# Second product of the attention terms on GpSimd, and the value matmuls turned around onto two column halves of TensorE

## The reference, cut to what matters

```
scores = q @ k.T / 8                      # 1024 x 1024, for each of 8 x 8 = 64 heads
scores = where(chaos(scores), scores / PHI, scores)
attn   = softmax(scores)
attn   = attn * (sin(C1 * attn) * exp(-attn * attn / PHI) + cos(C2 * attn))
ctx    = attn @ v ;  h = h + ctx @ Wo + bo
```

## Time and profile before

| | us |
|---|---|
| runs: median (lowest to highest) of 3 | 6793.55 (6787.77 to 19916.96) |
| the profiled execution | 6774.6 |
| its span, first to last instruction | 6772.9 |
| busy in the span: PE / VectorE / ScalarE / GpSimd | 5442.1 / 5082.3 / 4262.2 / 2754.5 |

### The profile page before, as it was taken

One profiled execution on the slowest core, in us unless ns is written; L12 is line 12 of the kernel. 1 busy time (PEld: TensorE's weight loads), 2 busy tenths in 40 slices (PEclk: granted clock), 3 DMA queues, 4 the chain that ended last, 5 costly groups with the idle time before them and its releaser, 6 DMA issues. The chain is left out here.

```text
span 6772.9 us, 115321 instructions
## 1 busy us (share of the span) xinstructions
PE 5442.1 (80%) x32426; PEld 3955.2 (58%) x32489; DVE 5082.3 (75%) x10177; ACT 4262.2 (63%) x7370; POOL 2754.5 (41%) x2639
## 2 busy tenths in 40 slices
PE   2788877787777877877888777778787799997999
PEld 1455555555555555555655555555555577775777
DVE  1888888888888888888888888888888555555443
ACT  1677777777777777777777777777777322222222
POOL 4445554444555544444555444445554200100111
PEclk9888898989889888888888889888988799898999
DMA  1000000000000000000000000000000000000000
GB/s 17 12 8 7 7 7 7 7 7 10 7 7 7 7 7 7 7 9 9 7 7 7 7 7 7 9 9 7 7 7 4 8 1 2 1 1 13 4 6 6
DMA packets 34500, 48.46 MB, mean 7 GB/s; under 512 B 24473, under 2 KB 24537, under 8 KB 34010
## 3 DMA queue, kind: packets, MB, share of 16 engines
q1 hardware_dynamic: 31962, 43.49, 2.5%
q0 software_dynamic: 2048, 0.14, 0.1%
HBM read 39.40 MB, written 4.19 MB: 6 GB/s over the span
## 5 line engine op out<-in xcount | busy, mean ns | idle before, releaser
L571 PE MATMUL banks<-ident,att 128*128 128x128 f32 x8192 | 1458.9, 311 | 873.6 <-DVE ag L508 496.8
L571 PEld LDWEIGHTS banks<-ident,att 128*128 128x128 f32 x8192 | 1024.2, 159 | 1568.6 <-DVE ag L508 1044.0
L377 POOL TENSOR_TENSOR sinb<-sinb,work 128x512 f32<-128x512 f32 x1024 | 1289.3, 1272 | 900.3 <-DVE sinb L482 898.3
L599 PE MATMUL banks<-kT,qT 128*128 128x512 f32 x2048 | 1262.5, 702 | 113.9 <-ACT att L423 104.0
L387 POOL TENSOR_SCALAR wgt<-wgt 128x512 f32<-128x512 f32 x1024 | 700.2, 684 | 1586.7 <-DVE wgt L502 1581.4
L635 PEld LDWEIGHTS outp<-vo,sinb 128*128 128x128 f32 x8192 | 1164.7, 216 | 214.9 <-issue 185.3
L635 PE MATMUL outp<-vo,sinb 128*128 128x64 f32 x8192 | 1162.6, 295 | 1.9 <-ACT att L423 1.9
L476 DVE TENSOR_TENSOR work<-banks,work 128x512 f32<-128x512 f32 x1024 | 699.8, 689 | 254.0 <-ACT work L435 183.6
L451 ACT ACTIVATE work<-banks 128x512 f32<-128x512 f32 x1024 | 609.9, 596 | 420.4 <-PE banks L571 411.6
L458 ACT ACTIVATE mag<-banks 128x512 f32<-128x512 f32 x1024 | 606.4, 594 | 356.2 <-PE banks L599 350.0
L435 ACT ACTIVATE work<-banks,halfpi 128x512 f32<-128x512 f32 x1024 | 695.4, 685 | 208.9 <-PE banks L571 139.6
(11 more groups left out here) (194 smaller groups left out, 6740.6 us busy)
## 6 DMA issues: line engine op xcount, KB each, us to landing
xq<-xT_dram SPq DMA_DIRECT2D x64, 256.0 KB
xv<-xT_dram SPq DMA_DIRECT2D x64, 256.0 KB, 3.7
xT_dram<-xT SPq DMA_DIRECT2D x8, 256.0 KB, 2.9
out<-hres SPq DMA_DIRECT2D x8, 256.0 KB, 2.6
base<-in_L_tok_turns,idx POOLq DMA_INDIRECT x64
wqk<-in_L_attn_Wq SPq DMA_DIRECT2D x64, 16.0 KB
wqk<-in_L_attn_Wk SPq DMA_DIRECT2D x64, 16.0 KB
wqk<-in_L_attn_bq SPq DMA_DIRECT2D x64, 0.2 KB
```

The lines of the kernel that those rows point to most:

```text
L377: nc.gpsimd.tensor_tensor(sinb[:, k % RING], sinb[:, k % RING], work[:, k % RING], ALU.add).then_inc(summed, 1)
L571: mm = nc.tensor.matmul(bank[:, i * P:(i + 1) * P], att[:, p, 4 * half + i, kt * P:(kt + 1) * P], ident[:], is_transpose=True, start=(i == ...
L599: nc.tensor.matmul(score_bank(n), qT[:, p, (n // 2) * P:(n // 2 + 1) * P], kT[:, p, (n % 2) * 512:(n % 2 + 1) * 512], start=True, stop=Tru ...
```

## The change

- `sinb` gets ScalarE's sine directly (it was left in the bank), GpSimd multiplies it by `ag` (SBUF times SBUF) in place of its sum, and VectorE's product of sine and `ag` is gone. `fill(k)` of the sine part now waits for ScalarE's sine of tile k-4.
- The sum of the two terms is not formed: `work` (cosine term) and `sinb` (sine term) both go through TensorE as the moving operand, 512 columns each, with `vo` (64 columns) stationary, into partitions 0 to 63 and 64 to 127 of `outp`. The result is transposed and lies in two halves; VectorE moves it into `acc` (a copy for even heads, an addition for odd ones), and after every second head eight matmuls with `pair` (two identities, one above the other) turn it back and add its halves; then VectorE adds it to `hres`.
- The order of the tiles is `kt` first within a query half (it was half first within `kt`), so `outp` holds one half of the queries at a time and is emptied twice a head, at steps 86 and 103. The value matmuls sit at steps 78 to 85 (one a step) and 88 to 102 (one every second step).
- `kT` has one buffer, its rows shared by the two parities; so the projections move from steps 18 and 20 to 24 and 26, the `vo` work from step 25 (of stage 1) to 29.

```
-        kT = sb("kT", [P, 2, S])
+        kT = sb("kT", [P, S])
+        acc = sb("acc", [P, 2, 512])
+        pair = sb("pair", [P, D])
...
-        PROJ, VAL = 18, 25 + STEPS
+        PROJ, VAL = 24, 29 + STEPS
-        AV = [SINE + 6 + 8 * k // 5 for k in range(NTILE)]
-        OUT = AV[-1] + 1
+        AV = [SINE + 6 + k if k < TB else SINE + 16 + 2 * (k - TB) for k in range(NTILE)]
+        OUT = (AV[TB - 1] + 1, AV[-1] + 1)
+        FOLD, ADD = OUT[1] + 1, OUT[1] + 2
...
# GpSimd
-                        k = a - SINE - 5
+                        k = a - SINE - 4
-                            wait(pool, tmul, NTILE * g + k + 1)
-                            nc.gpsimd.tensor_tensor(sinb[:, k % RING], sinb[:, k % RING], work[:, k % RING],
-                                                    ALU.add).then_inc(summed, 1)
+                            wait(pool, sined, NTILE * g + k + 1)
+                            wait(pool, agd, NTILE * (g + 1))
+                            nc.gpsimd.tensor_tensor(sinb[:, k % RING], sinb[:, k % RING], ag[:, k],
+                                                    ALU.mult).then_inc(tmul, 1)
...
# ScalarE, projections
-                    wait(act, qk, NTILE * (g - 1))
+                    wait(act, qk, NTILE * g)
-                nc.scalar.activation(qT[0:D, p, cols], outp[0:D], ACT.Copy, scale=QSCALE).then_inc(qk_sb, 1)
-                nc.scalar.activation(kT[0:D, p, cols], outp[D:P], ACT.Copy).then_inc(qk_sb, 1)
+                rows = slice(p * D, (p + 1) * D)
+                nc.scalar.activation(qT[rows, p, cols], outp[0:D], ACT.Copy, scale=QSCALE).then_inc(qk_sb, 1)
+                nc.scalar.activation(kT[rows, cols], outp[D:P], ACT.Copy).then_inc(qk_sb, 1)
...
# ScalarE, cosine and sine
-                                wait(act, summed, NTILE * g + k - RING + 1)
+                                wait(act, av, NTILE * g + k - RING + 1)
...
-                            nc.scalar.activation(sine_bank(k), sine_bank(k), ACT.Sin,
+                            wait(act, av, NTILE * g + k - RING + 1)
+                            nc.scalar.activation(sinb[:, k % RING], sine_bank(k), ACT.Sin,
...
# VectorE
-                        k = a - SINE - 4
-                            wait(dve, sined, NTILE * g + k + 1)
-                            wait(dve, av, NTILE * g + k - RING + 1)
-                            nc.vector.tensor_tensor(sinb[:, k % RING], sine_bank(k), ag[:, k],
-                                                    ALU.mult).then_inc(tmul, 1)
-                        if a == OUT:
-                            wait(dve, av, NTILE * (g + 1))
+                        if a in OUT:
+                            half = OUT.index(a)
+                            wait(dve, av, NTILE * g + TB * (half + 1))
+                            if p == 0:
+                                nc.vector.tensor_copy(acc[:, half], outp[:]).then_inc(evac, 1)
+                            else:
+                                nc.vector.tensor_tensor(acc[:, half], outp[:], acc[:, half], ALU.add).then_inc(evac, 1)
+                        if a == ADD and p == 1:
+                            wait(dve, folded, folds(g, p) + 1)
...
# TensorE
-                            wait(pe, turned, TB * (g + 1))
-                            kt, half = k // 2, k % 2
+                            wait(pe, turned, TB * g + 4 * (k // TB) + 4)
+                            kt, half = k % TB, k // TB
...
-                            fill(g, p, gauss_bank(d), d // 2, d % 2)
+                            fill(g, p, gauss_bank(d), d % TB, d // TB)
...
-                                wait(pe, tmul, NTILE * g + k - 3)
-                            fill(g, p, sine_bank(k), k // 2, k % 2)
+                                wait(pe, sined, NTILE * g + k - 3)
+                            fill(g, p, sine_bank(k), k % TB, k // TB)
...
-                            for i in range(4):
-                                o = (4 * half + i) * D
-                                mm = nc.tensor.matmul(outp[:, o:o + D], sinb[:, k % RING, i * P:(i + 1) * P],
-                                                      vo[:, kt, :], start=(k == 0 and i == 0),
-                                                      stop=(k >= NTILE - 2), skip_group_check=True)
+                            if k == TB:
+                                wait(pe, evac, 2 * g + 1)
+                            for term, rows in ((work, slice(0, D)), (sinb, slice(D, P))):
+                                mm = nc.tensor.matmul(outp[rows], vo[:, kt, :], term[:, k % RING],
+                                                      start=(kt == 0), stop=(kt == TB - 1), skip_group_check=True)
                             mm.then_inc(av, 1)
+                        if a == FOLD and p == 1:
+                            wait(pe, evac, 2 * g + 2)
+                            for j in range(TB):
+                                mm = nc.tensor.matmul(outp[:, j * D:(j + 1) * D],
+                                                      acc[:, j // 4, j % 4 * P:(j % 4 + 1) * P], pair[:],
+                                                      start=True, stop=True)
+                            mm.then_inc(folded, 1)
```

More of the change, by code:

```diff
@@ L277, in lattice @@
         names = ("consts loadq loadv projd qk_sb vald v_sb qk mags rounded kept factor filtered bias expd "
-                 "recip weights weights2 turned xpose squared gauss agd cosd acd nned sined tmul summed av outd").split()
+                 "recip weights weights2 turned xpose squared gauss agd cosd acd nned sined tmul av evac folded outd").split()
         (consts, loadq, loadv, projd, qk_sb, vald, v_sb, qk, mags, rounded, kept, factor, filtered, bias,
-         expd, recip, weights, weights2, turned, xpose, squared, gauss, agd, cosd, acd, nned, sined, tmul, summed,
-         av, outd) = (sem("l_" + n) for n in names)
+         expd, recip, weights, weights2, turned, xpose, squared, gauss, agd, cosd, acd, nned, sined, tmul,
+         av, evac, folded, outd) = (sem("l_" + n) for n in names)
         NTILE = 2 * TB
@@ L316, in stages, with folds @@
                     yield g, (par - stage) % 2, s + STEPS * stage
+        def folds(g, p):
+            if isinstance(g, int):
+                return g // 2
+            return (g - p) // 2
         def score_bank(n):
@@ L365, in _ @@
             pool.wait_ge(consts, 5)
-            nc.gpsimd.memset(qT[D:P], 0.0).then_inc(consts, 1)
+            nc.gpsimd.tensor_tensor(pair[:], ident[:, 0:D], ident[:, D:P], ALU.add).then_inc(consts, 1)
             pool.wait_ge(consts, 6)
-            nc.gpsimd.memset(kT[D:P], 0.0).then_inc(consts, 1)
+            nc.gpsimd.memset(qT[:], 0.0).then_inc(consts, 1)
+            pool.wait_ge(consts, 7)
+            nc.gpsimd.memset(kT[:], 0.0).then_inc(consts, 1)
             def iteration(t, par):
@@ L393, in _ @@
         def _(act):
[L394 removed]
+            act.wait_ge(consts, 8)
             def projections(g, p, c):
@@ L447, in iteration @@
                             if d < RING:
-                                wait(act, summed, NTILE * g - RING + d + 1)
+                                wait(act, av, NTILE * g - RING + d + 1)
                             else:
@@ L507, in iteration @@
                             wait(dve, gauss, NTILE * g + d + 1)
+                            wait(dve, tmul, NTILE * (g - 1) + d + 1)
                             nc.vector.tensor_tensor(ag[:, d], gauss_bank(d), work[:, d % RING],
@@ L549, in _, with project @@
         def _(pe):
-            pe.wait_ge(consts, 7)
-            def project(g, c):
+            pe.wait_ge(consts, 8)
+            def project(g, p, c):
                 wait(pe, loadq, 80 * (g + 1))
                 if c == 0:
-                    wait(pe, outd, g - 2)
+                    wait(pe, evac, 2 * (g - 2))
+                    wait(pe, outd, folds(g - 2, p))
                 else:
@@ L560, in project @@
                 nc.tensor.matmul(outp[:], wqk[:], xq[:, c * 512:(c + 1) * 512], start=True, stop=True).then_inc(projd, 1)
-            project(0, 0)
-            project(0, 1)
+            project(0, 0, 0)
+            project(0, 0, 1)
             def fill(g, p, bank, kt, half):
@@ L597, in iteration @@
                             if n == 3:
-                                wait(pe, tmul, NTILE * (g - 2) + 13)
+                                wait(pe, sined, NTILE * (g - 2) + 13)
                             nc.tensor.matmul(score_bank(n), qT[:, p, (n // 2) * P:(n // 2 + 1) * P],
-                                             kT[:, p, (n % 2) * 512:(n % 2 + 1) * 512],
+                                             kT[:, (n % 2) * 512:(n % 2 + 1) * 512],
                                              start=True, stop=True).then_inc(qk, 1)
@@ L610, in iteration @@
                             if d < 3:
-                                wait(pe, tmul, NTILE * (g - 1) + 14 + d)
```

(26 more changed lines are left out.)

3 lines of the change are left out of this document (1 added, 2 removed).

## The result

7027.28 us (7018.53 to 7039.49, 4 runs) against 6790.66: a ratio of 1.0353 [1.0331, 1.0375], slower. (One of the four runs of the kernel before took 19916.96 us; it is in the median of 6790.66 and left out of the ratio.) The forecast was 7060 in a range of 6740 to 7350. The total came out; its terms did not, and their errors mostly cancelled.

What follows compares the result with a forecast made beforehand. VectorE was taken to bound the scores and gauss part, a ring of four PSUM banks the sine part. Terms of +3.4, +0.5, +1.0, +0.34 and -0.6 gave +4.6 us a head, +288 over 62 heads: 7060 us, range 6740 to 7350.

Steps and rivals of the forecast that it cites:

- ring and pairs in the sine part: Sine part: eight steps with value matmul pairs at 2.05 us, three without at 1.25, +3.4 us a head; ninth pair +0.5.
- moved work: Projection copies and `vo` matmuls at later steps, around the sine part's start: +1.0 us a head, between 0 and +3.1.
- emptying, fold, GpSimd: Mostly the VectorE-bound stretch: emptying and residual +0.34 us a head, fold 0 (or +0.95), shorter first rounding -0.6.
- The bound by stretch: VectorE full in scores and gauss part, no engine in the sine part; removing VectorE's 702 us pays only there.
- The pairs: TensorE, sine part: two value matmuls into column halves take 1.29 us plus 0.08 for the change of kind, 1.37.
- only the second and the third record can run together: TensorE, a pair's four records of 0.43 us: one overlap only, so 3 x 0.43 = 1.29 us.
- The signs: Head about 84 us; sine fills 2.0 us apart at eight steps, else 1.25; records at 0, 0.43, 0.43, 0.86; TensorE never idle.
- Fully together: Rival, value pairs on TensorE: both halves overlap completely, 0.86 us a pair, +0.9 us a head, 6830 us; chance 0.20.
- In turn: Rival, value pairs on TensorE: halves do not overlap, 1.72 us a pair, +8.6 us a head, 7310 us; chance 0.28.
- The ring set free: Rival, sine part: pairs at most 0.54 us, GpSimd sets 1.25 us a tile, -3.2 us a head, 6575 us; chance 0.12.

Runs made afterwards that it cites:

- the kernel with one half: Changed kernel with both value terms summed into the same column half of `outp` (partitions 0 to 63), same output: 7475.21 us.
- its best form: Changed kernel with the moved work in its old steps, `mag2` of three buffers and seven PSUM banks in the sine part's ring: 6794.88 us, ratio 1.0025.

## Why the prediction was right, and where it was not

The slower kernel was forecast, and the total of 7060 was near; but that is luck in good part. Put by stretches, with the kernel with the moved work put back as the step between, a head changed like this (us):

| term | forecast | measured |
|---|---|---|
| ring and pairs in the sine part | +3.4 and +0.5 | -0.2 |
| moved work | +1.0 | +2.8 |
| emptying, fold, GpSimd | -0.3 | +1.2 |
| head | +4.6 | +3.8 |

- **The bound by stretch** held. VectorE's 605 us went without a gain, since the stretch in which VectorE is full kept its instructions.
- **The pairs** were the wrong term. With the moved work put back, the sine part is 26.3 us against 26.5: ring and pairs together cost nothing there. The step that failed is "only the second and the third record can run together". It took the two records of each term for places in one queue, three of which must follow each other; the trace has both terms side by side, first record with first and second with second, 0.48 us apart, so that a pair took 1.01 us and not 1.37. (The step of a tile was also added up wrongly: 0.22 + 0.49 + 1.37 is 2.08, not 2.06.) The sum also took 1.25 us for steps without a pair and no gain at the start of the ring.
- **The moved work** was mis-sized the other way: +1.0 us a head (0 to 3.1) against 2.8 in the changed kernel and 3.3 in the kernel before. The projections' copies cost about the +1.2 that stood in the working, but nothing was absorbed, and the `vo` matmuls were counted at full clock and as if ScalarE could pass them; they cost 2.0.
- **Emptying, fold, GpSimd** were +0.34 and -0.6. The rest of a head in the kernel with the work put back is 54.5 against 53.2: +1.2, so this sum was too low. The fold, costed at nothing (or 0.95 a head "if not"), is the reason. It falls into every second head, and the heads can be sorted by it: without a fold the rest is 53.2 us, as in the kernel before; with one it is 55.7 (in the changed kernel 53.3 and 55.6). In one head of the changed kernel it takes TensorE 3.30 us to the next start, at a granted clock of 0.50. VectorE stands idle for it, and then again for the score tile whose matmul stood behind it in TensorE's queue:

```profile
2067.89 3.51 PE L659 MATMUL outp<-pair,acc 128*128 128x64 f32 x16
2071.19 1.06 PE L587 MATMUL banks<-ident,att 128*128 128x128 f32 x4
...
2071.63 0.69 DVE L501 TENSOR_TENSOR hres<-outp,hres 128x512 f32 x1 [0.58 <-PE outp L659]
2074.63 0.43 DVE L511 TENSOR_SCALAR wgt<-mag 128x512 f32<-128x512 f32 x1 [2.31 <-ACT mag L471]
```

That is the stretch in which VectorE is the bound, so what it waits there is lost. No run leaves the fold alone out. VectorE's first rounding does take 0.43 us instead of 1.04 (at 2048.31, behind GpSimd's scaling that ends at 2048.23), but in the heads without a fold the rest is no shorter than before, so this and the further emptying of `outp` come to nothing together.
- **The signs.** A head of 83.5 us against "about 84" and TensorE without idle time came as named; steps of 2.0 us and records at 0, 0.43, 0.43 and 0.86 did not (1.78 us, and 0, 0.01, 0.48 and 0.49).
- **The rivals.** "Fully together" described the pairs best (1.63 us a step against 1.78) and still had the wrong total, because the moved work was in it at +1.0 and the fold at nothing. "In turn" is what the kernel with one half measures in its pairs (1.86 us). "The ring set free" fails on the pairs at 1.01 us, where it needed 0.54; that there was something to gain in the sine part is what the kernel before with seven banks shows.

The forecast of 7060 was thus nearly the right total of partly wrong terms: of +4.6 us a head ring and pairs were 4.1 too dear, the moved work 1.8 and the rest 1.5 too cheap, which leaves the +3.8 of the traces.

The drain that the Trainium skill ("TensorEngine Tiling (Array Packing)", "Key Properties") announces for a change of tiling mode is bounded here: 1.01 us for a pair that would stream in 0.86, so at most 0.15 us for both changes, into the halves and back.

## What to carry to other kernels

Before an engine is relieved, look for what holds its result: here four PSUM banks did, and three banks that another stage left idle gave 3.1%, where a rewritten data path gave nothing even in its best form. A small block of work in a stretch where another engine is full (the fold) costs that engine every wait that it causes. Small work that a rewrite pushes out of its place (eight matmuls, four copies) is to be priced at its new place, with the in-order queue behind it and the clock that TensorE has there. And where a sum is given up, its operands' buffers live until the next reader: count that ring too.

## What the runs showed of the hardware

- Two float32 matmuls of 512 columns into the two column halves take 1.01 us together until a full-width matmul starts, and 1.86 in one half (2011.64 to 2013.50). Each leaves two records, and the first records of both start 0.01 us apart. (A float32 transpose of a fill leaves one record: x4 for four.)
- A VectorE product with both inputs in SBUF takes 0.69 us while GpSimd is idle and mostly 1.38 beside GpSimd's two-input operation; with one input in PSUM it takes 0.69. The Trainium skill ("GPSIMD Engine Reference", "Specifications") says that GpSimd's SBUF interfaces are shared with VectorE, with contention for VectorE instructions with two SBUF inputs, and the trace agrees.
- The sixteen records of the same eight matmuls span 1.90 us at a granted clock of 1.00 and 3.47 to 3.52 us at 0.50: 1.6 us is the clock's.
